# Decayed token sums in four scans of 256 instead of eight of 128, at every fourth step of the schedule

## The reference

```
x = x + conv_ref(group_norm(x))
t = tokens(x)
t = t + attn_ref(layer_norm(t))
t = t + ffn_ref(layer_norm(t))
...
def attn_ref(x, W_qkv, W_out, b_out):
    q, k, v, t = split(x @ W_qkv, 4)          # 8 heads of 16 channels
    out1 = softmax(q k^T * scale) v
    tg = abs(pos[None, :] - pos[:, None])
    attn2 = exp(-tg / e); attn2 = attn2 / attn2.sum(-1)
    out2 = attn2 t
    return concat(out1, out2) @ W_out + b_out
```

## Time and profile before

| what | value |
|---|---|
| time, median of 3 runs | 2376.35 us (2370.98 to 2392.26) |
| the profiled execution's own time | 2371.68 us |
| its span, first to last instruction | 2369.9 us |
| PE busy | 2076.4 us, 88% |
| DVE busy | 1897.7 us, 80% |
| ACT busy | 1460.3 us, 62% |
| POOL busy | 1019.7 us, 43% |
| mean granted PE clock | 0.936 of full speed |

### The profile page before, as it was taken

One profiled execution on the slowest core, in us unless ns is written; L12 is line 12 of the kernel. 1 busy time (PEld: TensorE's weight loads), 2 busy tenths in 40 slices (PEclk: granted clock), 3 DMA queues, 4 the chain that ended last, 5 costly groups with the idle time before them and its releaser, 6 DMA issues.

```text
span 2369.9 us, 35246 instructions
## 1 busy us (share of the span) xinstructions
PE 2076.4 (88%) x11552; PEld 962.0 (41%) x11552; DVE 1897.7 (80%) x3669; ACT 1460.3 (62%) x2897; POOL 1019.7 (43%) x1479
## 2 busy tenths in 40 slices
PE   2699999999999999999999999999999378777743
PEld 1233343433333343334334333333433156666633
DVE  5768799999999999999999999999881366676732
ACT  1127777777777777777787777777674134344410
POOL 2101224444342444434344443433333646777764
PEclk9999999999999999999999999999995688999965
DMA  5330322323132222313222232312012277666659
GB/s 172 55 50 1 55 46 47 91 38 79 29 76 46 47 53 40 76 29 78 46 47 52 41 73 34 77 37 47 15 51 84 77 234 257 205 204 209 209 186 339
DMA packets 100990, 215.06 MB, mean 91 GB/s; under 512 B 30224, under 2 KB 50392, under 8 KB 100376
## 3 DMA queue, kind: packets, MB, share of 16 engines
q1 hardware_dynamic: 78000, 166.96, 28.7%
q0 software_dynamic: 17280, 35.95, 4.3%
q10 hardware_dynamic: 5528, 9.91, 1.2%
HBM read 104.30 MB, written 61.23 MB: 70 GB/s over the span
## 4 chain that ended last, share of the span: by engine, by line
PE 59%; DVE 16%; POOL 8%; DMA 6%; issue 5%; ACT 4%; SPq 1%; ACTq 1%; POOLq 0%; DVEq 0%
PE ps L881 22%; PE ps L893 18%; DVE row_max L1420 11%; POOL y_dram L767 7%; PE ps L860 3%; PE ps L837 2%; ACT region L1170 2%; DMA y_dram<-region 2%; DMA big<-w_dram 2%; DMA region<-y_dram 2%; DVE region L1471 2%; PE ps L845 2%; PE ps L849 2%; PE ps L912 1%; PE ps L925 1%
## 5 line engine op out<-in xcount | busy, mean ns | idle before, releaser
L1420 DVE TENSOR_REDUCE row_max<-ps 128x1 f32<-128x512 f32 x2048 | 1292.3, 680 | 133.4 <-PE ps L860 117.0
L1170 ACT ACTIVATE region<-ps 128x512 f32<-128x512 f32 x2048 | 1093.5, 602 | 377.6 <-PE ps L881 373.0
L860 PE MATMUL ps<-big 48*128 48x512 f32 x2048 | 836.8, 479 | 32.6 <-DMA big<-k_parts 14.7
L881 PE MATMUL ps<-big 50*128 50x512 f32 x2048 | 781.2, 463 | 25.9 <-ACT region L1170 15.0
L881 PEld LDWEIGHTS ps<-big 50*128 50x128 f32 x2048 | 325.9, 191 | 655.9 <-ACT region L1170 505.2
L893 PE MATMUL ps<-region 128*32 128x512 f32 x4096 | 569.7, 629 | 0.0
L860 PEld LDWEIGHTS ps<-big 48*128 48x128 f32 x2048 | 346.3, 193 | 131.8 <-DVE row_max L1420 100.1
L767 POOL DMA_INDIRECT y_dram<-region x284 | 272.0, 958 | 120.0 <-issue 82.6
L713 POOL DMA_INDIRECT xs_dram<-region,slot x256 | 249.2, 974 | 81.2 <-issue 71.8
L649 POOL TENSOR_TENSOR norm_v<-norm 128x8 f32<-128x8 f32 x32 | 6.7, 210 | 573.4 <-DVE norm L1409 573.4
L1021 PE MATMUL ps<-big 128*128 128x512 f32 x284 | 125.9, 443 | 73.2 <-DMA big<-w_dram 72.7
(11 more groups left out here) (183 smaller groups left out, 2032.1 us busy)
## 6 DMA issues: line engine op xcount, KB each, us to landing
big<-w_dram SPq DMA_DIRECT2D x71, 514.0 KB, 4.6
big<-q_parts SPq DMA_DIRECT2D x384, 64.0 KB, 2.4
big<-k_parts SPq DMA_DIRECT2D x372, 64.0 KB, 2.4
region<-xs_dram SPq DMA_DIRECT2D x71, 264.0 KB, 2.9
region<-y_dram SPq DMA_DIRECT2D x16, 1024.0 KB, 10.0
region<-in_x SPq DMA_DIRECT2D x28, 512.0 KB, 5.2
t_dram<-region SPq DMA_DIRECT2D x16, 512.0 KB, 3.4
out<-region ACTq DMA_DIRECT2D x16, 512.0 KB, 6.0
```

Of the source, the lines that this page charges most:

```text
L860: pe.matmul(ps[:, M_BANK + half % M_BANKS, :], lane_rows(q_stack[k % 2], h, SHIFT_ROW)[:, t * P:(t + 1) * P], lane_rows(k_stack[k % 2], h, ...
L881: pe.matmul(ps[:, E_BANK + score % E_BANKS, :], lane_rows(k_stack[k % 2], h, STACK)[:, t * P:(t + 1) * P], lane_rows(q_stack[k % 2], h, ST ...
L1170: act.activation(probs[:, u % 2, step_head(k, s, i), :], ps[:, E_BANK + score % E_BANKS, :], ACT.Exp, scale=DH ** -0.5).then_inc(exp_done, 1)
L1420: dve.tensor_reduce(row_max[:, c, h * TILES + t:h * TILES + t + 1], ps[:, M_BANK + half % M_BANKS, :], AX.X, ALU.max).then_inc(max_done, 1)
```

## The change

Each direction runs in four scans of 256 tokens instead of eight of 128. The forward scans move from the steps 8, 10, ... 22 to 9, 13, 17, 21, the backward scans from 28, 30, ... 42 to 29, 33, 37, 41. The functions are the same; their loops over pieces, the ranges of columns and the count that `add_decayed` waits for follow from `PIECES`.

```
-PIECES = 8
+PIECES = 4
 PIECE = TOK // PIECES
...
-AT_FORWARD = tuple(range(8, 24, 2))
-AT_BACKWARD = tuple(range(28, 44, 2))
+AT_FORWARD = tuple(range(9, 25, 4))
+AT_BACKWARD = tuple(range(29, 45, 4))
```

## The result

Over 20 runs of each kernel, side by side on the same chip, the median went from 2370.94 us (2361.4 to 2392.26) to 2386.45 us (2371.55 to 2403.14): a ratio of 1.0063 with a 95% interval of 1.0041 to 1.0085. The change makes the kernel slower by 0.6%, where 0.5% faster was forecast. That lies within the 1% called "no change" in the chances, but on the other side of none, and the time lies above the range. The profiled execution took 2383.83 us with a span of 2382.0, 12.1 longer than the one of before. The ratios in this document leave out runs of over 1.5% above the fastest of their kernel, two of ten in `clear_keys`, two of ten in its repeat and none elsewhere; with them in, these two mean ratios would be some 0.9975 where 0.9953 and 0.9955 are given.

A forecast was written before the change was run, and what follows sets the result against it. DVE was taken to bound steps 30 to 43, with PE close. Savings of 16 x (0.5 + 0.1) = 9.6 plus 3.2 from the clock, 12.8 off 2371.7, gave 2358; own range 2347 to 2370, whole range 2340 to 2380.

The forecast's parts named there:

- What bounds the kernel: DVE and PE run neck and neck; DVE's chain bounds steps 30 to 43, so scans count in full there.
- The price of a piece: A scan of 256 was taken as 0.79 alone, 0.71 of DVE's time, between 0.61 and 0.95.
- I add 0.2 for a wait in step 37: Step 37's backward scan falls into POOL's last key pieces; 0.2 added, the wait lying between 0 and 0.73.
- `logits_out` "and all behind it": With the first backward scan moved to step 29 these come 0.5 later; a wait absorbs half, leaving +0.25.
- I price all three at nothing: Work behind moved scans, `logits_out` freeing the side bank, step 13's `add_attention`: each zero, at most 0.5 to 0.7.
- The largest is in step 13: Largest forward-half surplus in one step, 0.71 + 0.66 for `add_attention`, against about 1.2 us that three banks hold.
- the steps 34, 38 and 42: Sign of a right forecast: these steps would be closest to PE.
- The forward half: Steps 8 to 25: DVE saves 0.28, mostly hidden by PE; 0.1 an image counted, between 0 and 0.28.
- The clock: After the logits PE's clock falls, 1.58 each; two fewer falls taken, -3.2, between -12.6 and +9.5.
- The sum: 16 x (0.5 + 0.1) = 9.6 and 3.2 for the clock make 12.8 saved; 2358 forecast.
- Nothing gained: Rival: little fixed part in a scan, or bursts costing PE what lighter steps give; 2370, chance 0.18.
- the first rival: Step 9's first forward scan held behind POOL's power, costing PE 1.2 an image; +9.6, 2381, chance 0.10.

The follow-up runs named there:

- clear_keys: Changed kernel with the last two backward scans in steps 39 and 43 in place of 37 and 41; 2364.97 us, 0.9953 of the kernel before.
- keys_later_x_first: Changed kernel with POOL's keys split held until step 37's scan is done and SP issuing the next image's load first; 2369.66 us, 1.0006 of before.
- after_again: The changed kernel measured once more on the same chip, nothing edited; 2385.55 us, 1.007 of the kernel before.
- clear_keys_pick_even: Changed kernel with backward scans in 29, 33, 39, 43 and parts of the choice in even steps 30 to 42; 2374.52 us, 1.0012 of before.
- keys_later: Changed kernel with POOL's split of the keys held until the third backward scan (step 37) is done; 2395.54 us, 1.0101 of before.
- even4: Changed kernel with its four scans each way on even steps (8, 12, 16, 20 and 28, 32, 36, 40); 2365.16 us, 0.9981 of before.
- odd8: Changed kernel with eight scans of 128 each way, on odd steps 9 to 23 and 29 to 43; 2391.81 us, 1.0089 of before.
- odd4_pick_even: Changed kernel with the parts of the choice of experts one step earlier, in 30, 32, ... 42; 2366.58 us, 0.9972 of before.

## Why the prediction was wrong

**What bounds the kernel: right for before, and only in part after.** What is won or lost in steps 30 to 43 shows in the image's time. But the chain there, DVE's throughout before, is PE's from 1169.42 to 1176.68 after the change. Where DVE gets lighter PE bounds, and then the places count in which DVE frees no bank for long.

**The price of a piece: right.** 0.74 undisturbed where 0.79 was taken; the scans' total fell by 27.5 us, some 25 being forecast, with some luck: cheaper pieces and a longer wait in step 37 partly cancel. The first backward scan took 1.02, that is 0.28 of waiting behind L663 where 0.3 was taken.

**The step that failed: "I add 0.2 for a wait in step 37".** It was given as between 0 and 0.73, and 0.2 was taken without a working. The scan asks at 1177.88, about where the last of the keys' pieces begins (1175.86 + 3 x 0.70), and in thirteen images alike; it waited 0.59 each time. `keys_later_x_first` shows that this wait is passed on to PE in full, 0.63 an image, and that the step-41 falls go with it: without it the ratio is 1.0006, with it 1.0063.

**What made it worse, and was put at nothing: step 31.** The prediction has `logits_out` "and all behind it" come later, and asks only for the price of the delay, not what the work behind it then meets. The first part of the choice met POOL's split of the queries: L1504 took 0.71 in place of 0.21, PE waited 0.51 in place of 0.18, and pairs 34-35 grew by 0.34. That this wait makes that growth is argued from the kernels' order above; it was not taken away alone.

**"I price all three at nothing": about right.** In step 37 the choice adds 0.48 to the 1.26 of the waiting scan. But with the scan undisturbed (`keys_later_x_first`) PE waits 0.20 and 0.31 behind the scan and choice of steps 37 and 41, about what it waited there before, 0.35 and 0.23. `add_decayed` starts earlier and meets L1522, which went from 0.42 to 0.68. That pairs 44-45 grew, from 3.39 to 3.66, is hardly its doing: PE's wait at 1186.93 lies in them, ahead of L1522.

**"The largest is in step 13": wrong.** Pairs 12-13 and 14-15 take 3.38 and 3.37, within 0.01 of before. The largest surplus is in step 37, 1.74, and the next in step 31, 1.64, where 1.2 was given as what three banks hold. The measure was useful but was tried on the wrong step, and without the waits behind POOL. PE's waits stand in steps 33, 39 and 43, next to the steps 34, 38 and 42 that were named as closest to PE.

**The forward half: gained 0.2** in pairs 10-11, within its bounds, and gave it back in pairs 34-35.

**The clock: wrong sign.** Two fewer falls were forecast behind the logits; the profiles have seven there before and after (the prediction's eighth slow stretch belongs to a long one that begins ahead of its logits), and three more came in a place that had none. In `after_again` there are eight and four. A step that leaves PE idle was not asked what the clock does behind it.

**The sum.** Forecast were 0.6 less for an image; the change gave 0.39 more. Of this miss of 0.99 the wait behind the keys is 0.63 (`keys_later_x_first`) and pairs 34-35 some 0.33. Without the two an image would be some 0.57 shorter than before, an estimate from these two figures: the saving was sized about rightly and lost at two steps. `clear_keys`, where the keys' wait is gone, gave 0.75 less and 0.5% in all. Of the 26 us between forecast and profile (2383.8 - 2358) the image accounts for 16 x 0.99 = 16, and the falls, 3.2 gained on paper and some 5.5 lost in the loop, for about 9.

**The rivals.** The first fell. The power and the scan beside it, in order of time of all engines:

```profile
1131.39 1.68 POOL L657 TENSOR_TENSOR norm_v<-norm_v,minus_half 128x8 f32<-128x8 f32 x1
1131.52 0.68 DVE L1458 TENSOR_TENSOR_SCAN region<-fade,region 128x256 f32<-128x256 f32 x1
```

The scan begins 0.13 after the power and ends well inside it. The Trainium skill, "SBUF — State Buffer", section "Who interferes with whom", would have held it out; the trace agrees with that rule for L676 (0.74 becomes 1.33) and not for this power. *Nothing gained* named the mechanism, bursts that cost PE what the lighter steps give, but priced it as a draw: it kept the forecast's 0.2 for the wait and had no effect on the clock. The slower end of the range was set by the first rival alone. The upper ends of three costs that follow one another at one step, the wait (0.53 x 13 = 6.9), the choice behind it (0.5 x 16 = 8.0) and the clock (9.5 + 3.2 = 12.7), would have led from 2358 to 2386. That this is near the measured time is partly luck: the second hardly came, and the wait in step 31, which did, is not among them.

What stays open: why only some images fall in step 41 after the same wait of 0.79, what lengthens the falls in `clear_keys_pick_even`, and what step 31's wait costs alone. The falls themselves were not steered in any run.

## What to carry to other kernels

When a piece of work moves to a step, list what every other engine runs in that step, and do the same for work that only slips with it. Where both partners come at fixed steps, price a wait at the moment that the schedule gives, up to its upper bound, not at some middle value. Ask of each step how long the consumer leaves all buffers full, the longest stretch and not the mean; fewer and longer pieces pay only where the longest stretch doesn't grow. The best version here came from one constant: `AT_BACKWARD = (29, 33, 39, 43)`, 0.5% faster than the kernel before.

## What the runs showed of the hardware

A wait of PE of 0.79 us was followed, some 2 us after it, by the lower clock (0.50 over 551.8 to 558.4) in three of thirteen images of after, and not in the others. In `keys_later` waits of 1.31 to 1.90 were followed by it in all five images that had them. Waits of 0.20 behind the third backward scan (`keys_later_x_first`, `clear_keys`), of 0.40 in `even4` and of 0.50 in `clear_keys_pick_even` were followed by it in none. But in `odd8`, with 0.52 there and in some images 1.05 some 10 us earlier, it came in four, and in `odd4_pick_even`, with 0.51 to 0.79, in two.

Operations of DVE stretched beside POOL's pieces of 128 x 256: a scan from 0.74 to 1.33 and L1504 from 0.21 to 0.71 beside L676, L1522 from 0.14 to 0.68 beside L698. Beside the power at L657 a scan took 0.68.

And an image can be shorter by 1.4 us (101.93 against 103.34) with no gain in the whole, when the stretches at the lower clock grow, as in the one granted 0.53 over eleven microseconds.
